# A fused router, FFN and masking kernel: the last pair's second tile masks two terms ahead of the shared sum, and the first weights are rounded on another engine

## What is computed

```python
base = jnp.einsum('btd,od->bto', x, W)
lora_out = jnp.einsum('bter,bte,eor->bto', h, gates, B)
cond = base + SCALING * lora_out
...
dots = jax.nn.softmax(x @ centroids.T / TEMPERATURE, axis=-1)
hits = dots > THRESHOLD
query_sel = jnp.any(hits, axis=1)
cluster_sel = jnp.any(hits, axis=0)
row_sel = cluster_sel[assignments]
dense = x @ weight.T + bias
out = jnp.where(query_sel[:, None] & row_sel[None, :], dense, 0)
return x + out
```

## Time and profile before

| what | value |
|---|---|
| median of 3 runs | 337.38 us (336.47 to 337.40) |
| the profiled execution's own time | 337.06 us |
| its span, from first to last instruction | 335.2 us |
| PE busy in the span | 329.8 us (98%) |
| DVE busy | 260.4 us (78%) |
| ACT busy | 139.6 us (42%) |
| transfers, mean | 146 GB/s |

### The profile page before, as it was taken

One profiled execution on the slowest core, in us unless ns is written; L12 is line 12 of the kernel. 1 busy time (PEld: TensorE's weight loads), 2 busy tenths in 40 slices (PEclk: granted clock), 3 DMA queues, 4 the chain that ended last, 5 costly groups with the idle time before them and its releaser, 6 DMA issues.

```text
span 335.2 us, 4613 instructions
## 1 busy us (share of the span) xinstructions
PE 329.8 (98%) x1758; PEld 289.9 (86%) x1758; DVE 260.4 (78%) x472; ACT 139.6 (42%) x235; POOL 1.0 (0%) x9
## 2 busy tenths in 40 slices
PE   8999999999999999999999999999999999999995
PEld 7888888999999999999877888888888888888885
DVE  3747966567898889889996979679397594993967
ACT  4834745445657655765633313232233322231220
POOL 1000000000000000000000000000000000000000
PEclk9999999999999999999999999999999999999999
DMA  7975351333533433325612271804508237061113
GB/s 219 408 224 199 145 190 64 125 128 125 183 98 132 155 127 125 127 98 222 246 38 89 117 259 77 280 21 188 190 1 296 81 134 241 0 212 41 63 65 125
DMA packets 14358, 49.10 MB, mean 146 GB/s; under 512 B 1728, under 2 KB 1984, under 8 KB 14336
## 3 DMA queue, kind: packets, MB, share of 16 engines
q1 hardware_dynamic: 14336, 48.80, 40.9%
HBM read 40.41 MB, written 8.39 MB: 146 GB/s over the span
## 4 chain that ended last, share of the span: by engine, by line
PE 93%; DVE 5%; issue 1%; ACT 0%; POOL 0%; POOLq 0%; DVEq 0%
PE ps L984 25%; PE ps L986 24%; PE ps L985 24%; PE ps L1051 7%; PE ps L993 7%; PE ps L1053 3%; PE ps L990 1%; DVE xt_lo L612 1%; PE ps L1062 1%; DVE u L953 0%; PE ps L1069 0%; DVE u L879 0%; PE ps L1071 0%; DVE hg L742 0%; DVE hits L766 0%
## 5 line engine op out<-in xcount | busy, mean ns | idle before, releaser
L984 PE MATMUL ps<-vt_hi,w_hi 128*128 128x288 f32 (+1 forms) x184 | 58.7, 319 | 0.0
L986 PE MATMUL ps<-vt_hi,w_lo 128*128 128x288 f32 (+1 forms) x184 | 58.0, 315 | 0.0
L985 PE MATMUL ps<-vt_lo,w_hi 128*128 128x288 f32 (+1 forms) x184 | 58.0, 315 | 0.0
L409 ACT ACTIVATE u<-ps 128x512 f32<-128x512 f32 x32 | 19.1, 597 | 83.7 <-PE ps L986 57.0
L985 PE MATMUL ps<-gop_lo,sl_s_hi 128*128 128x512 f32 x128 | 49.8, 389 | 0.0
L1051 PE MATMUL ps<-aw,xt_hi 128*128 128x400 f32 x128 | 38.9, 365 | 0.0
L984 PE MATMUL ps<-gop_hi_t,sl_s_hi 128*128 128x512 f32 x96 | 37.4, 390 | 0.0
L986 PE MATMUL ps<-gop_hi_t,sl_s_lo 128*128 128x512 f32 x96 | 37.3, 389 | 0.0
L985 PEld LDWEIGHTS ps<-vt_lo,w_hi 128*128 128x128 f32 x184 | 34.6, 188 | 1.6
L984 PEld LDWEIGHTS ps<-vt_hi,w_hi 128*128 128x128 f32 x184 | 34.5, 188 | 1.6
L986 PEld LDWEIGHTS ps<-vt_hi,w_lo 128*128 128x128 f32 x184 | 34.5, 188 | 1.6
(11 more groups left out here) (135 smaller groups left out, 662.1 us busy)
## 6 DMA issues: line engine op xcount, KB each, us to landing
xt_raw<-in_xt SPq DMA_DIRECT2D x32, 512.0 KB, 3.7
nat<-in_x SPq DMA_DIRECT2D x16, 512.0 KB, 4.0
out<-nat SPq DMA_DIRECT2D x15, 512.0 KB, 2.7
w_raw<-in_w SPq DMA_DIRECT2D x8, 512.0 KB, 3.3
wraw<-in_w SPq DMA_DIRECT2D x6, 512.0 KB, 3.9
vt_raw<-in_v SPq DMA_DIRECT2D x4, 576.0 KB, 5.1
vt_raw<-in_v SPq DMA_DIRECT2D x4, 256.0 KB, 5.2
wq_raw<-in_wq SPq DMA_DIRECT2D x4, 256.0 KB, 5.4
```

The lines of the kernel that those rows point to most:

```text
L409: return nc.scalar.activation(dst, src, ACT.Copy)
L984: nc.tensor.matmul(dst, l_hi, r_hi, start=start, stop=False, skip_group_check=True)
L985: nc.tensor.matmul(dst, l_hi, r_lo, start=False, stop=False, skip_group_check=True)
L986: return nc.tensor.matmul(dst, l_lo, r_hi, start=False, stop=stop, skip_group_check=True)
```

## The change

Three edits.

1. **Start, PE.** The warm-up is 9 matmuls of 512 columns in bf16 on a tile of zeros (`warm`) in place of 19 f32 transposes of the identity. DVE fills the tile as its first instruction (`warm_ready`), and PE waits for that and no longer for POOL's identity. The wait for the identity moves to the first real transpose (`turn_hg`).
2. **Start, DVE and ACT.** For piece 0, DVE rounds W (`tensor_copy` into `wq_hi`, `wq0_hi`), and ACT rounds only V. DVE then makes V's lo and W's lo as before. Pieces 1 to 5 are as before, with counts shifted by one.
3. **End, last pair, tile b.** ACT no longer copies X after P3 out of its bank. DVE masks P4 (from bank V) and P5 (from u3) ahead, adds them to `nat` half by half, then waits for X, masks X from its bank for both halves in one instruction (the 512 columns are read twice), and `finish` adds it.

```diff
-WARM_UP = 19
+WARM_UP = 9
...
+            act.wait_ge(v1_landed[0], 16)
+            copy(vt1_hi[:, 0, :], vt1_raw[:, 0, :]).then_inc(v1_hi, 1)
+            for p in range(1, len(STEPS)):
...
-                act.wait_ge(x_bank, 3 * i + 3)
-                keep(2, BANK_X, i, result[1], u3_kept)
+                if i + 1 < NPAIR:
+                    act.wait_ge(x_bank, 3 * i + 3)
+                    keep(2, BANK_X, i, result[1], u3_kept)
...
+            nc.vector.memset(warm[:], 0.0).then_inc(warm_ready, 1)
+
+            dve.wait_ge(wq_landed[0], 16)
+            nc.vector.tensor_copy(wq_hi[:, 0, :], wq_raw[:, 0, :]).then_inc(wq0_hi, 1)
+            dve.wait_ge(v1_hi, 1)
+            rest(vt1_lo[:, 0, :], vt1_raw[:, 0, :], vt1_hi[:, 0, :]).then_inc(v1_split, 1)
+            dve.wait_ge(wq0_hi, 1)
+            rest(wq_lo[:, 0, :], wq_raw[:, 0, :], wq_hi[:, 0, :]).then_inc(wq_split, 1)
...
-            add22(i)
-            add21(i)
-            mask(i, 1)
+
+            dve.wait_ge(v_bank, i + 1)
+            masked_to(1, u[:, 2, :], bank(i, BANK_V), halves[:, 0]).then_inc(ahead, 1)
+            dve.wait_ge(p5_kept, i + 1)
+            masked_to(1, u[:, 3, :], u[:, 3, :], halves[:, 1]).then_inc(ahead, 1)
+            dve.wait_ge(ahead, 1)
+            dve.wait_ge(based[1], i + 1)
+            minus(at_b[:, f1], at_b[:, f1], u[:, 2, :]).then_inc(ahead, 1)
+            dve.wait_ge(ahead, 2)
+            nc.vector.tensor_tensor(at_b[:, f2], u[:, 3, :], at_b[:, f2], ALU.add).then_inc(ahead, 1)
+            dve.wait_ge(ahead, 4)
+            dve.wait_ge(x_bank, 3 * i + 3)
+            masked_to(1, u[:, 2:4, :], bank(i, BANK_X).unsqueeze(1).broadcast_to([P, 2, HALF]),
+                      halves).then_inc(masked[1], 1)
             finish(i, 1)
...
-            pe.wait_ge(const_ready, 2)
+            pe.wait_ge(warm_ready, 1)
             for _ in range(WARM_UP):
-                nc.tensor.transpose(ps[:, 0, 0:P], ident[:], ident[:])
+                nc.tensor.matmul(ps[:, 0, :], warm[:, 0:P], warm[:], start=True, stop=True)
...
-            pe.wait_ge(wq_hi_done, 1)
+            pe.wait_ge(wq0_hi, 1)
...
+                if n == 0:
+                    pe.wait_ge(const_ready, 2)
```

More of the change, by code:

```diff
@@ L117, in adaln_ffn_kernel @@
         hgt_all = sb("hgt_all", [P, NT * P], F32)
+        with nc.sbuf_tensor("warm", [P, HALF], BF16) as warm:
+            pass
         gop_raw, gop_lo = sb_split("gop", [P, 7, KH, HALF])
@@ L183, in adaln_ffn_kernel @@
         wq_landed = [sem(f"wq_landed{p}") for p in range(len(STEPS))]
+        wq0_hi = sem("wq0_hi")
         wq_hi_done = sem("wq_hi_done")
@@ L206, in adaln_ffn_kernel @@
         const_ready = sem("const_ready")
+        warm_ready = sem("warm_ready")
+        ahead = sem("ahead")
         setup_step = sem("setup_step")
@@ L437, in t_part @@
                 copy(gop_hi_t[:, :, jj, :], gop_raw[:, T1:T4 + 1, jj, :]).then_inc(t_hi, 1)
-            for p in range(len(STEPS)):
+            act.wait_ge(v1_landed[0], 16)
+            copy(vt1_hi[:, 0, :], vt1_raw[:, 0, :]).then_inc(v1_hi, 1)
+            for p in range(1, len(STEPS)):
                 split_first(p)
@@ L625, in split_first @@
                 rest(vt1_lo[:, j, :], vt1_raw[:, j, :], vt1_hi[:, j, :]).then_inc(v1_split, 1)
-                dve.wait_ge(wq_hi_done, p + 1)
+                dve.wait_ge(wq_hi_done, p)
                 rest(wq_lo[:, j, :], wq_raw[:, j, :], wq_hi[:, j, :]).then_inc(wq_split, 1)
@@ L948, in _, with masked_to @@
             f1, f2 = slice(0, HALF), slice(HALF, FO)
[L949 to L954, removed]
+            at, at_b = nat[i % 2][0], nat[i % 2][1]
+            halves = mask_row[:].rearrange("p (h f) -> p h f", h=2)
+            def masked_to(c, dst, src, of):
+                return nc.vector.scalar_tensor_tensor(out=dst, in0=src, scalar=qsel[:, 2 * i + c:2 * i + c + 1],
+                                                      in1=of, op0=ALU.mult, op1=ALU.mult)
             base(i, 0)
             dve.wait_ge(p1_kept, i + 1)
-            masked_to(u[:, 0, :], u[:, 0, :], f1).then_inc(masked[0], 1)
+            masked_to(0, u[:, 0, :], u[:, 0, :], halves[:, 0]).then_inc(masked[0], 1)
             base(i, 1)
@@ L969, in _ @@
             dve.wait_ge(sum12, i + 1)
-            masked_to(u[:, 1, :], u[:, 1, :], f2).then_inc(masked[0], 1)
+            masked_to(0, u[:, 1, :], u[:, 1, :], halves[:, 1]).then_inc(masked[0], 1)
             dve.wait_ge(masked[0], i + 2)
@@ L976, in _ @@
                 dve.wait_ge(y_bank, i + 1 + h)
-                masked_to(u[:, 0, cols], bank(i + h, BANK_Y)[:, cols], cols).then_inc(masked[0], 1)
+                masked_to(0, u[:, 0, cols], bank(i + h, BANK_Y)[:, cols], mask_row[:, cols]).then_inc(masked[0], 1)
                 dve.wait_ge(masked[0], i + 3 + h)
```

## The result

| | median | lowest to highest | runs |
|---|---|---|---|
| before | 336.97 us | 336.32 to 337.41 | 22 |
| with the change | 336.38 us | 335.83 to 337.03 | 22 |

The ratio is 0.9981, 95% interval 0.9975 to 0.9987: faster by 0.19%, clear of zero, and less than the 0.3% from which the forecast spoke of faster. The predicted 336.2 is 0.2 off, inside the range. The gain of 0.6 us, though, is half of the 1.2 that I had forecast against the 337.38 then shown: 22 runs put before 0.4 lower than those three did. The sum had been made against a profiled execution of 337.06, and forecast 0.84 less than that. The measured gain of 0.59 is 0.25 smaller, and before's median of 336.97 is 0.09 lower than 337.06: the two partly cancel, so that the time forecast looks better than the gain forecast was. The profiled execution took 336.48 us, its span is 334.7.

A forecast was written before the change was run, and what follows sets the result against it. PE, fed almost without a gap, bounds the kernel, so only its two ends can gain: 337.06 - 0.45 (end) - 0.39 (start) = 336.22, say 336.2 us. The range was 335.6 to 337.0.

The forecast's parts named there:

- The reading of what bounds the kernel: PE, fed almost without a gap, holds 93% of the chain of waits; gains can come only from the two ends.
- The end, 0.45: DVE's last add in the last pair ends at 332.54 instead of 332.99: gain 0.45 us, bounds 0.20 and 0.50.
- the first 0.2 of it the ahead work takes: At the end, masks and adds ahead of X take the first 0.2 of the 1.3 us of instructions removed.
- Rival (c): The end gives only 0.2 because ahead work and bank mask cost 0.7 more; 336.5 us, chance 0.06.
- The start, 0.39: Earlier warm-up and W rounding start PE's real work at 5.16 and piece 1 at 8.52 instead of 8.91: gain 0.39 us.
- the 0.64 us lost to the lower level: Piece 0's real matmuls on PE lose 0.64 us at the lower clock level, where before they lost 0.70.
- If the rise keeps its distance from PE's first activity: At the start, the clock rise comes 0.42 us earlier, following the earlier warm-up on PE.
- Its W lo ends at 7.38 + 0.69 = 8.07: Piece 1's W lo on DVE ends at 8.07, unmoved by the change, so PE can't start piece 1 before about 8.25.
- the cap of 0.66: The most the start can give: piece 1 at 8.25 instead of 8.91, 0.66 us.
- (a): Start: dense warm-up matmuls raise the clock before real work; start gives 0.66, total 335.95 us, chance 0.20.
- (b): The start gives 0.0 to 0.15, from a 0.69 copy or an unmoved or later clock rise; 336.5 to 336.6, chance 0.17.
- (d): Start: zero products don't raise the clock, so the rise waits for real work; slower, 338.0 us, chance 0.07.

The follow-up runs named there:

- the doubled mask: The changed kernel with the mask of X from its bank done twice in DVE's last chain; its single run took 336.17 us.
- by part: The changed kernel with PE taking pieces 1 to 3 as hi by hi, hi by lo, lo by hi, each with its own wait; 335.94 us, again 335.83.
- e3_warm_only: The kernel before with only the nine zero matmuls as warm-up, ACT still rounding W's first piece, old end; 337.14 us, ratio 1.0005.

## Why the prediction was right or wrong

**The reading of what bounds the kernel: right.** Only the two ends moved. Between piece 1's start and PE's last result lie 322.58 to 322.75 us in all fourteen profiles, whatever the edit.

**The end, 0.45: right, shown.** Measured 0.47 with both edits and with edit 3 alone. The mask that reads a bank twice cost the lower bound, 1.28. The two cuts that I had named are the two waits that appeared, 0.40 at bank W and 0.53 at the last quarter. One remark beside the sum was wrong: "the first 0.2 of it the ahead work takes". By its own numbers add12 could have started 329.08 - 327.55 = 1.53 sooner, more than the 1.3 of instructions taken off, since the wait for ACT's copy of X went too; bank W then takes 0.45 of that and PE's end 331.60 - 330.97 = 0.63, which leaves the 0.45. Rival (c) is refuted: the four instructions and the mask cost what was taken for them, and the doubled mask shows that even 0.7 us of dearer work would have been covered by the 1.1 us of room.

**The start, 0.39: the direction right, the size too large.** The durations were right, and so was the first real matmul. The term that failed is the 0.64 us lost to the lower level, and with it the fixed cap:

- "If the rise keeps its distance from PE's first activity." In the profiled pair it did not: 5.2 us from the first transpose before, 5.6 from the first zero matmul with the change, so that the piece took 8.79 - 5.22 = 3.57 us, 0.85 more than 12 x 0.23 = 2.72, and not 0.64 more; with the first real matmul at 5.22 in place of 5.16 this is the whole of the 0.27 between 8.79 and 8.52. Among all profiles the distance goes from 3 to 5.6 us with zeros and ones, and from 3.7 to 5.2 with transposes. A rise of one profile is one draw; a start 0.33 us sooner moves it less than it scatters.
- "Its W lo ends at 7.38 + 0.69 = 8.07, from transfers that the change doesn't move." The change doesn't, but each execution does, by up to a microsecond. So the cap of 0.66 is no fixed cap, and in four of the six profiles with both start edits and the old order W's lo came last. Taking the pieces by part removes this end and gave about 0.3 us more, which shows that it held. What makes the landing of the first pieces scatter was not tested.

Over 22 runs each the start is worth what is left of the medians' difference, 0.59 - 0.47 = 0.12; with the nine further runs of the changed kernel, about 0.2. Both lie below my 0.39 and inside its bounds of 0 to 0.66. The interval of the ratio, 0.44 to 0.84 us in all, leaves the start -0.03 to 0.37, and the start edits alone gave 0.30 with an interval that holds zero: the size is known no better than that. That the profile before had a late rise is luck of the draw: its 8.91 is the latest start of piece 1 among the three profiles with transposes (8.91, 8.88, 8.41).

**The reference.** The sum was made against the profiled 337.06, which was right; the chance of "faster" I then read against 337.38, the median of three. With a spread of 1.1 us, three runs put a median no better than some tenths. Against 337.06 my own sum was -0.25% and no more than "same": I should have given that the larger share. The 0.55 for faster went to a case that didn't come, the 0.38 to the one that did.

**The rivals.** (a) Dense matmuls raise the clock before the real work: it happens, in six of the ten profiles with dense warm-up matmuls, but also in one of the three with transposes. Its 335.95 did not come: with an early rise W's lo of piece 1 mostly ends last, and before has early rises of its own. The profile with edit 3 alone has the old warm-up, and its transposes speed up at the end (ns, min/median/max):

```profile
L1003 PE MATMUL ps<-ident x19: 272/421/476, 1.5 to 5.3; 128*128 128x128 f32 x19
```

The minimum, 272, is the duration that the earlier trace rows show at the higher level, the trace's clock record begins at 5.24, and the first real matmul starts only at 5.57. So transposes alone, before any real matmul, were enough, and the sentence of the Trainium skill that I weighed (TensorE: Matmul & The Clock Gate, Part 4, transposes don't count as PE-busy the same way) does not hold for these f32 transposes, as far as the clock goes. Whether dense matmuls raise it sooner on average stays open: three profiles with transposes and ten with dense ones scatter too widely, and the times of e3_warm_only (337.14) give no sign of it. (b) The start gives little: its rise part is what came, its dear copy wasn't. (d) Zeros don't raise the clock: refuted, zeros and ones alike, while no warm-up at all costs 1.6 us.

## What to carry to other kernels

An instruction taken off an engine's last chain is worth the distance to the next bound, not its duration: read what the chain will meet (here bank W and the last quarter's bank, where DVE came to wait 0.40 and 0.53 us) before adding up. A start that is read from one profile is one draw of a race, between the clock's rise and the landing of the first pieces; look at which of the two ends can be taken out of the race, as asking for the hi parts first did, rather than moving the one that the single profile shows. And state a gain of 0.2% against a median of twenty runs, not of three.

## What the runs showed that I had not expected

- The rise of TensorE's clock between its two levels, 1.2 and 2.4 GHz, scatters by over 2 us from one execution to another: from 4.1 us (in the profile of the doubled mask, during its last zero matmuls) to about 6.8, with the same warm-up. The clock record of a trace begins only with the rise, so the table by stretches gives a granted clock of 1.00 for the microseconds before it too; only the matmuls' distances show the lower level there.
- W's lo of piece 1, behind the same four first transfers, ended between 7.6 and 9.1 us.
- A fill of the same 128 by 512 bf16 tile took 0.27 us with zeros, which the row shows issued as 256 elements of four bytes, and 0.48 with ones, issued as 512 elements of bf16:

```profile
0.91 0.48 DVE L665 MEMSET warm<- 128x512 bf16 x1 [0.91 <-PEq L1287]
```

- A mask with an operand of PSUM that is read twice by its access pattern costs the same 1.28 us as one from SBUF.
